# Issuing the value matmuls of a latent attention two key tiles at a time

## The chip, the cores and the metric

One Trainium2 chip, one of its cores. The metric is the device time of one execution in microseconds (us); the kernel before was run three times.

## The reference

Four pairs of an attention-like layer and a feed-forward-like layer on x of shape (2, 1024, 256) with a context of shape (2, 77, 256). The change touches only the first attention ("latent attention", stage A of the kernel), in which x supplies the queries and both the context and x itself supply keys and values:

```python
q = ln @ Wq                                   # ln: normed x, 1024 rows in each of 2 batches
kv = concatenate([xn, ln], axis=-2) @ Wkv     # xn: normed context, 77 rows; 1101 keys
k, v = split(kv, 2, axis=-1)                  # 16 heads of 64
logits = einsum('bhld,bhsd->bhls', q * scale, k * scale)
w = softmax(logits)
out = einsum('bhls,bhsd->bhld', w, v)
out = out.transpose(0, 2, 1, 3).reshape(B, L, INNER) @ Wo
```

## The kernel before, in words

Stage A takes some 1,130 us of the span; the stages behind it (three mixtures of experts, three other attentions, an alignment, soft slots) are untouched.

The stage runs 16 **units**, n = 0 to 15, one for each pair of heads (8) in each batch b (2). Each engine has its own queue, written out by hand, and they meet at semaphores. In a unit the 1101 keys are walked in KT = 9 **key tiles** kt (eight of 128, the last of 77). Scores are made with keys on the partitions and 1024 queries on the free axis, so that a key tile of two heads j makes four **halves** of 512 queries; a half is two matmuls (L395, L397) into one of three PSUM banks, and ScalarE takes it through Exp into `probs` (L483). `probs` is a ring of RING = 3 key tiles.

- **TensorE (PE)**, `body` (L368), in order: for each key tile the four halves, and behind them work for the same or other units. `values(n, b, kt)` (L337) waits until a key tile's four halves are through Exp and issues its four matmuls (L344: two blocks of 512 queries by two heads; each is a 64-column matmul in f32, in the trace two records and two weight loads, so 8 records for a key tile) into banks 4 and 5, where they accumulate over the nine key tiles. Before the change `values(kt - 1)` follows the halves of key tile kt, and `values(KT - 1)` closes the unit. `denominators` (L350, matmuls L356) then sums `key_sums` over partitions, again with 64 columns.
- Between the halves PE also does the work of the **next unit** m = n + 1: `project_q` at kt 0 (L270), `project_k` and `project_ctx` at (2, 0) (L270, L290, L293), `project_v` at kt 2, j = 1 (L302; it waits for `k_lo` from VectorE), and from kt 3 on two **maxima** pieces behind each half (`more`, L376; matmul L316): 48 pieces of 367 keys, whose largest score VectorE finds. They go through three banks, so a piece waits until the third one back is reduced. Behind the last piece `rows(m)` (L320) turns the maxima over. At kt 1 the output projection of the unit before, `leave` (L324, matmuls L333), has its two parts c = 0 and 1.
- **VectorE (DVE)**: the low parts of q (L512) and copies (L515), adding the output of the unit before to x (`add`, L543, which releases `x_added`), the low part of k (L521, releases `k_lo`), copies of k (L529, releases `k_second`), 48 reductions (L532), one over their results (L535), and the division by the denominator (`heads`, L555).
- **ScalarE (ACT)**: the exponentials, the high parts of q and k (L441, L446), copies of v (L456), the DMA that lays the maxima's rows out (L462), and Ln and Exp of the denominators (L498, L501) after `denominators`. `project_q` of the next unit waits for that Ln.
- **GpSimd (POOL)**: one addition for each head and key tile from kt 1 on into `key_sums` (L587), 16 in a unit. ScalarE may overwrite a place in the ring only when the values and the sum that read it are done (L478, L479).

`project_k` of unit m of 2 and more waits for `x_added` (L284), so for the second `add` of unit n - 1. Unit 0 has no `leave`; unit 15 has no next unit, so no projections and no maxima.

Of the kernel before, what the change touches and what calls it, by code (L numbers as in the profile page):

```python
# [171 lines left out]
def wait(engine, semaphore, value):  # L172

    if not isinstance(value, int) or value > 0:
        engine.wait_ge(semaphore, value)


def latent_attention(nc, consts, x, a, ctx_n, w_qkv, w_o, slots_zeroed):
# [14 lines left out]
    KT = S // P + 1  # L193
    QT = S // P
    UNITS = 2 * QT
    RING = 3
    assert PIECE * 3 == KEYS and PIECE % 2
    OWN = [slice(0, DH), slice(DH, P)]
    OTHER = [slice(DH, P), slice(0, DH)]
# [4 lines left out]
    with ExitStack() as stack:  # L204
# [7 lines left out]
        v_tok = sc.sb("v_tok", [P, 2, KT, P])  # L212
        probs = sc.sb("probs", [P, 2, RING, S])
        key_sums = sc.sb("key_sums", [P, 2, S])
# [51 lines left out]
        def _(pe):  # L266
# [7 lines left out]
            def project_q(m, b):  # L274
                if b == 0:
                    pe.wait_ge(s["in_loaded"], 8 * m + 16)
                wait(pe, s["logden_ready"], 2 * m - 2)
                project(0, b).then_inc(s["q_ps"], 1)

            def project_k(m, b):  # L280
                if isinstance(m, int) and m < 2:
                    pe.wait_ge(s["q_lo"], 2 * m + 2)
                else:
                    pe.wait_ge(s["x_added"], 2 * m - 2)  # L284
                project(1, b).then_inc(s["k_ps"], 1)

            def project_ctx(m, b):

                for c in range(C):
                    pe.matmul(ps[:, 3, 0:CTX], wqkv[:, 1, c, :], ctx_n[:, c, b * CTX:(b + 1) * CTX],  # L290
                              start=c == 0, stop=c == C - 1)
                for c in range(C):
                    mm = pe.matmul(ps[0:CTX, 3, P:2 * P], ctx_n[:, c, b * CTX:(b + 1) * CTX], wqkv[:, 2, c, :],  # L293
                                   start=c == 0, stop=c == C - 1)
                mm.then_inc(s["ctx_ps"], 1)

            def project_v(m, b):

                pe.wait_ge(s["k_lo"], 2 * m + 2)
                for kt in range(KT - 1):  # L300
                    for c in range(C):
                        mm = pe.matmul(bank_pair(6)[:, kt * P:(kt + 1) * P], a[:, c, b * S + kt * P:b * S + (kt + 1) * P],  # L302
                                       wqkv[:, 2, c, :], start=c == 0, stop=c == C - 1)
                mm.then_inc(s["v_ps"], 1)

            def maxima(m, b, first, count):

                for i in range(first, min(first + count, PIECES)):
                    j, qt = divmod(i // 3, QT)
                    if i == 0:  # L310
                        pe.wait_ge(s["k_second"], 2 * m + 2)
                    elif i < 3:
                        pe.wait_ge(s["v_ready"], m + 1)
                    else:
                        pe.wait_ge(s["piece_max"], PIECES * m + i - 2)
                    pe.matmul(ps[:, MAX_BANKS[i % 3], 0:PW], q_one[:, b, j, qt * P:(qt + 1) * P],  # L316
                              k_one[:, b, j, (i % 3) * PIECE:(i % 3) * PIECE + PW], start=True, stop=True)\
                      .then_inc(s["piece_ps"], 1)

            def rows(m):  # L320
                pe.wait_ge(s["nmax_ready"], m + 1)
                pe.transpose(ps[0:UNITS, 7, 0:P], nmax[:, :], consts["ident"][:, :]).then_inc(s["rows_ps"], 1)

            def leave(n, c, q_after=None):  # L324

                if c == 0:
                    pe.wait_ge(s["heads_ready"], n + 1)
                    if q_after is not None:
                        pe.wait_ge(s["q_lo"], 2 * q_after + 2)
                else:  # L330
                    pe.wait_ge(s["x_added"], 2 * n + 1)
                for blk in range(2):
                    mm = pe.matmul(ps[:, 6 + blk, :], wo[:, c * P:(c + 1) * P], heads[:, blk * BLK:(blk + 1) * BLK],  # L333
                                   start=True, stop=True)
                mm.then_inc(s["y_ps"], 1)

            def values(n, b, kt):  # L337

                pe.wait_ge(s["exp_ready"], 4 * KT * n + 4 * kt + 4)
                if kt == 0:  # L340
                    wait(pe, s["heads_ready"], n)
                for blk in range(2):
                    for j in range(2):
                        mm = pe.matmul(ps[DH * j:DH * j + DH, 4 + blk, :], v_tok[:, b, kt, DH * j:DH * j + DH],  # L344
                                       probs[:, j, kt % RING, blk * BLK:(blk + 1) * BLK],
                                       start=kt == 0, stop=kt == KT - 1)
                        if (blk, j) == (1, 1):
                            mm.then_inc(s["pv_ps"], 1)
# [19 lines left out]
            def body(n, b, first, last):  # L368
                m, mb = n + 1, 1 - b
                if b == 1:  # L370
                    pe.wait_ge(s["out_loaded"], 8 * n + 8)
                pe.wait_ge(s["row_ready"], 32 * n + 32)
                pe.wait_ge(s["k_second"], 2 * n + 2)
                done = 0

                def more():  # L376

                    nonlocal done
                    if not last and kt >= 3 and done < PIECES:
                        maxima(m, mb, done, 1)  # L380
                        done += 1
                        if done == PIECES:
                            rows(m)

                for kt in range(KT):
                    kw = P if kt < KT - 1 else CTX
                    for j in range(2):
                        for blk in range(2):
                            cols = slice(blk * BLK, (blk + 1) * BLK)
                            half = 4 * kt + 2 * j + blk  # L390
                            if half >= 3:
                                pe.wait_ge(s["exp_ready"], 4 * KT * n + half - 2)
                            else:
                                wait(pe, s["exp_ready"], 4 * KT * n)
                            pe.matmul(ps[0:kw, half % 3, :], k_one[:, b, j, kt * P:kt * P + kw], q_one[:, b, j, cols],  # L395
                                      start=True, stop=False)
                            pe.matmul(ps[0:kw, half % 3, :], k_two[:, b, j, kt * P:kt * P + kw], q_two[:, b, j, cols],  # L397
                                      start=False, stop=True).then_inc(s["score_ps"], 1)
                            more()
                            more()  # L400
                        if (kt, j) == (0, 0) and not last:
                            project_q(m, mb)
                        if kt == 1 and not first:
                            leave(n - 1, j, None if last else m)
                        if (kt, j) == (2, 0) and not last:
                            project_k(m, mb)
                            project_ctx(m, mb)
                        if j and kt:
                            values(n, b, kt - 1)
                        if (kt, j) == (2, 1) and not last:  # L410
                            project_v(m, mb)
                if not last:
                    kt = KT
                    while done < PIECES:
                        more()
                values(n, b, KT - 1)
                if last:
                    pe.wait_ge(s["x_added"], 2 * n)
                denominators(n)
                if last:  # L420
                    leave_last(n)
# [10 lines left out]

            pe.wait_ge(s["zeroed"], 7)
            units(pe, body, prologue)

        @block.scalar
        def _(act):
# [34 lines left out]
            def body(n, b, first, last):  # L472
                m, mb = n + 1, 1 - b
                for kt in range(KT):
                    kw = P if kt < KT - 1 else CTX
                    for j in range(2):
                        if kt >= RING:
                            act.wait_ge(s["pv_ps"], KT * n + kt - RING + 1)  # L478
                            act.wait_ge(s["summed"], 2 * (KT - 1) * n + 2 * max(kt - RING, 1))  # L479
                        for blk in range(2):  # L480
                            half = 4 * kt + 2 * j + blk
                            act.wait_ge(s["score_ps"], 4 * KT * n + half + 1)
                            act.activation(probs[0:kw, j, kt % RING, blk * BLK:(blk + 1) * BLK], ps[0:kw, half % 3, :],  # L483
                                           ACT.Exp, scale=1.0 / 8.0).then_inc(s["exp_ready"], 1)
# [2005 lines left out]
```

## Time and profile before

| | |
|---|---|
| median of 3 runs | 4280.51 us (4279.39 to 4281.56) |
| profiled execution, its own time | 4283.65 us |
| its span | 4281.7 us |
| PE busy | 3114.4 us (73%) |
| DVE busy | 2152.2 us (50%) |
| ACT busy | 1510.2 us (35%) |
| POOL busy | 1037.0 us (24%) |

The busy shares are means over all stages. What a change to stage A is worth has to be read inside one of its units, from the order of the timeline there and from which wait ends last. A record of a matmul shows a modelled end; starts, and the gap from one weight load to the next, are the better measure. "PE" rows are matmuls, "PEld" rows weight loads.

### The profile page before, as it was taken

The numbers are of one execution on the slowest core, as the hardware profiler recorded it, in microseconds if no ns is written. First come the engines' busy times: TensorE is split into PE (matmuls) and PEld (weight loads), VectorE is DVE, ScalarE is ACT, GpSimd is POOL, SyncE is SP. The second block draws the span as 40 slices with busy tenths as digits, with TensorE's granted clock in tenths as the row PEclk, the third lists the DMA queues.
The fourth block names the chain that finished last, engine by engine and source line by source line (L and its number), as shares of the span: only waits on it lengthen the run. The fifth ranks groups of instructions, "written<-read, shape, count | busy, mean of one in ns | idle before, by whom it ended". The sixth has DMA issues, their size and how long they took to land. (4 is left out here: it accounts for less than half of the span.)

```text
span 4281.7 us, 41469 instructions
## 1 busy us (share of the span) xinstructions
PE 3114.4 (73%) x14046; PEld 1867.5 (44%) x14046; DVE 2152.2 (50%) x3679; ACT 1510.2 (35%) x2290; POOL 1037.0 (24%) x625
## 2 busy tenths in 40 slices
PE   4899999999965576397585888988469530069769
PEld 1554545455434343397252444443259510034344
DVE  3655556555513262376364767765247543721270
ACT  2344444444433234264132344555236210022230
POOL 0355556455532120301131000000220312001110
PEclk7899999999977787698697899999679765579899
DMA  2000000000004200464100000000056324110260
GB/s 84 4 6 1 5 5 5 5 0 5 2 10 143 63 1 1 149 219 140 34 0 10 3 2 3 5 2 1 31 180 221 101 23 52 6 24 30 81 234 20
DMA packets 92601, 204.72 MB, mean 48 GB/s; under 512 B 31146, under 2 KB 65578, under 8 KB 83739
## 3 DMA queue, kind: packets, MB, share of 16 engines
q0 software_dynamic: 18512, 109.48, 7.5%
q1 hardware_dynamic: 69946, 86.94, 7.5%
q10 hardware_dynamic: 3984, 6.29, 0.4%
q8 instruction: 88, 1.44, 0.1%
q14 instruction: 71, 0.57, 0.0%
HBM read 154.41 MB, written 48.01 MB: 47 GB/s over the span
## 5 line engine op out<-in xcount | busy, mean ns | idle before, releaser
L587 POOL TENSOR_TENSOR A_key_sums<-A_key_sums,A_probs 128x1024 f32<-128x1024 f32 (+1 forms) x224 | 526.9, 2372 | 253.4 <-ACT A_probs L483 253.4
L483 ACT ACTIVATE A_probs<-A_banks 128x512 f32<-128x512 f32 (+1 forms) x576 | 329.4, 597 | 413.2 <-PE A_banks L397 411.0
L532 DVE TENSOR_REDUCE A_part_max<-A_banks 128x1 f32<-128x367 f32 x768 | 354.0, 531 | 156.8 <-PE A_banks L316 155.4
L1629 ACT ACTIVATE F_probs<-F_banks 128x512 f32<-128x512 f32 x512 | 272.1, 601 | 356.9 <-PE F_banks L1577 343.0
L1686 DVE TENSOR_REDUCE F_part_max<-F_banks 128x1 f32<-128x512 f32 x512 | 319.2, 684 | 47.3 <-PE F_banks L1533 46.5
L395 PE MATMUL A_banks<-A_q_one,A_k_one 128*128 128x512 f32 (+1 forms) x576 | 256.8, 446 | 26.7 <-ACT A_probs L483 23.3
L344 PE MATMUL A_banks<-A_probs,A_v_tok 128*64 128x512 f32 x1152 | 275.6, 604 | 0.0
L1533 PE MATMUL F_banks<-F_k_split,F_q_split 128*128 128x512 f32 x512 | 233.3, 480 | 35.6 <-DVE F_k_split L1678 34.1
L316 PE MATMUL A_banks<-A_k_one,A_q_one 128*128 128x368 f32 x768 | 230.0, 382 | 6.8 <-ACT A_v_tok L456 6.4
L1577 PE MATMUL F_banks<-F_q_split,F_k_split 128*128 128x512 f32 x512 | 211.2, 444 | 23.7 <-ACT F_probs L1629 19.4
L1996 PE MATMUL G_banks<-G_path,G_ctx_rows 77*128 77x512 f32 x16 | 14.0, 1071 | 294.2 <-DMA G_ctx_rows<-in_G_ctx_rows 294.2
L397 PE MATMUL A_banks<-A_q_two,A_k_two 128*128 128x512 f32 (+1 forms) x576 | 227.3, 395 | 0.0
L161 POOL TENSOR_SCALAR F_r<-F_r,F_ln_w 128x512 f32<-128x512 f32 x16 | 28.8, 1818 | 786.6 <-DVE F_r L126 786.6
L316 PEld LDWEIGHTS A_banks<-A_k_one,A_q_one 128*128 128x128 f32 x768 | 147.3, 192 | 94.6 <-DVE A_part_max L532 58.4
L1533 PEld LDWEIGHTS F_banks<-F_k_split,F_q_split 128*128 128x128 f32 x512 | 100.6, 201 | 181.0 <-DVE F_part_max L1686 112.6
L395 PEld LDWEIGHTS A_banks<-A_q_one,A_k_one 128*128 128x128 f32 (+1 forms) x576 | 106.5, 185 | 140.0 <-issue 96.0
L1546 PE MATMUL F_banks<-F_probs,F_v_tok 128*32 128x512 f32 x1024 | 149.4, 658 | 15.9 <-ACT F_probs L1629 15.9
L270 PE MATMUL A_banks<-g_y,A_wqkv 128*128 128x512 f32 x256 | 122.2, 622 | 30.7 <-DVE A_part_max L570 26.0
L587 POOL TENSOR_TENSOR A_key_sums<-A_probs 128x1024 f32<-128x1024 f32 x32 | 75.9, 2373 | 281.5 <-ACT A_probs L483 281.5
L834 PE MATMUL F_banks<-F_y_hi,F_w_split 128*128 128x256 f32 x736 | 130.1, 290 | 11.9 <-DVE F_w_split L993 11.9
L834 PE MATMUL D_banks<-D_y_hi,D_w_split 128*128 128x256 f32 x736 | 130.1, 290 | 11.9 <-DVE D_w_split L993 11.9
L1996 PEld LDWEIGHTS G_banks<-G_path,G_ctx_rows 77*128 77x128 f32 x16 | 5.2, 335 | 302.3 <-DMA G_ctx_rows<-in_G_ctx_rows 295.1
(532 smaller groups left out, 6432.0 us busy)
## 6 DMA issues: line engine op xcount, KB each, us to landing
H_w<-in_H_w SPq DMA_DIRECT2D x16, 1024.0 KB, 7.1
moe_in<-A_zeros ACTq DMA_DIRECT2D x1, 5888.0 KB, 17.4
D_tile_in<-moe_in SPq DMA_DIRECT2D x23, 256.0 KB, 5.4
moe_out<-D_z SPq DMA_DIRECT2D x23, 256.0 KB, 5.1
F_tile_in<-moe_in SPq DMA_DIRECT2D x23, 256.0 KB, 5.4
moe_out<-F_z SPq DMA_DIRECT2D x23, 256.0 KB, 5.0
slots<-H_staged SPq DMA_DIRECT2D x8, 512.0 KB, 4.1
made<-H_made POOLq DMA_DIRECT2D x16, 256.0 KB, 6.3
```

Of the source, the lines that this page charges most:

```text
L316: pe.matmul(ps[:, MAX_BANKS[i % 3], 0:PW], q_one[:, b, j, qt * P:(qt + 1) * P], k_one[:, b, j, (i % 3) * PIECE:(i % 3) * PIECE + PW], star ...
L344: mm = pe.matmul(ps[DH * j:DH * j + DH, 4 + blk, :], v_tok[:, b, kt, DH * j:DH * j + DH], probs[:, j, kt % RING, blk * BLK:(blk + 1) * BLK ...
L395: pe.matmul(ps[0:kw, half % 3, :], k_one[:, b, j, kt * P:kt * P + kw], q_one[:, b, j, cols], start=True, stop=False)
L397: pe.matmul(ps[0:kw, half % 3, :], k_two[:, b, j, kt * P:kt * P + kw], q_two[:, b, j, cols], start=False, stop=True).then_inc(s["score_ps" ...
L483: act.activation(probs[0:kw, j, kt % RING, blk * BLK:(blk + 1) * BLK], ps[0:kw, half % 3, :], ACT.Exp, scale=1.0 / 8.0).then_inc(s["exp_re ...
L532: dve.tensor_reduce(part_max[:, i // 3, i % 3:i % 3 + 1], ps[:, MAX_BANKS[i % 3], 0:PIECE], AX.X, ALU.max).then_inc(s["piece_max"], 1)
L587: pool.tensor_tensor(key_sums[0:kw, j, :], before, probs[0:kw, j, kt % RING, :], ALU.add).then_inc(s["summed"], 1)
L834: mm = pe.matmul(ps[:, 1 + pairs * (n % 2) + pair, at * SLOT:(at + 1) * SLOT], weight_in(i, w_part, pair, c, QM * q + at), part[:, i % 2, ...
L1533: mm = pe.matmul(bank, q_split[:, mb, hd // 2, qt * P:(qt + 1) * P], k_split[:, mb, hd, kb * BLK:(kb + 1) * BLK], start=True, stop=True)
L1577: pe.matmul(ps[:, k % 3, :], k_split[:, b, hd, kt * P:(kt + 1) * P], q_split[:, b, hd // 2, blk * BLK:(blk + 1) * BLK], start=True, stop=T ...
L1629: act.activation(probs[:, i % RING, hd, :], ps[:, k % 3, :], ACT.Exp, scale=DH ** -0.5).then_inc(s["exp_ready"], 1)
L1686: op = dve.tensor_reduce(part_max[:, i // QB, i % QB:i % QB + 1], bank, AX.X, ALU.max)
```

## The change

The value matmuls of two key tiles are issued together, behind the halves of key tiles 3, 5 and 7, and those of the last three key tiles at the end of the unit. Since a key tile's probabilities are then read up to three key tiles later, the ring holds six of them. No instruction is added or removed.

```diff
@@ -193,7 +193,9 @@
-    RING = 3
+    RING = 6
+    VALUES_BEHIND = {3: (0, 1), 5: (2, 3), 7: (4, 5)}
+    VALUES_LAST = (6, 7, 8)
@@ -405,15 +407,17 @@
                             project_k(m, mb)
                             project_ctx(m, mb)
-                        if j and kt:
-                            values(n, b, kt - 1)
+                        if j:
+                            for done_kt in VALUES_BEHIND.get(kt, ()):
+                                values(n, b, done_kt)
                         if (kt, j) == (2, 1) and not last:
                             project_v(m, mb)
                 if not last:
                     kt = KT
                     while done < PIECES:
                         more()
-                values(n, b, KT - 1)
+                for done_kt in VALUES_LAST:
+                    values(n, b, done_kt)
```

## Rows read from the trace of the kernel before

**Rows 1.** Windows: stage A; us, then busy (instructions) by engine, PE clock, DMA.

```profile
95.00:1210.00 1115.00, 1025.03 (x4225) 551.38 (x4225) 612.06 (x1005) 490.25 (x780) 602.79 (x256) 0.98 0.01 4
```

**Rows 2.** Groups by line, stage A: count, busy, mean ns, idle before and releaser.

```profile
L587 POOL TENSOR_TENSOR A_key_sums<-A_key_sums,A_probs 128x1024 f32<-128x1024 f32 (+1 forms) x224 | 526.9, 2372 | 253.4 <-ACT A_probs L483 253.4
L532 DVE TENSOR_REDUCE A_part_max<-A_banks 128x1 f32<-128x367 f32 x768 | 354.0, 531 | 156.8 <-PE A_banks L316 155.4
```

**Rows 3.** Timeline of VectorE, the heads multiplication that closes each unit: start, us.

```profile
482.88 1.22 DVE L555 TENSOR_TENSOR A_heads<-A_banks,A_rden 128x1024 f32<-128x1024 f32 x1 [8.55 <-ACT A_rden L501]
552.38 1.22 DVE L555 TENSOR_TENSOR A_heads<-A_banks,A_rden 128x1024 f32<-128x1024 f32 x1 [8.55 <-ACT A_rden L501]
620.18 1.23 DVE L555 TENSOR_TENSOR A_heads<-A_banks,A_rden 128x1024 f32<-128x1024 f32 x1 [8.55 <-ACT A_rden L501]
...
1165.79 1.23 DVE L555 TENSOR_TENSOR A_heads<-A_banks,A_rden 128x1024 f32<-128x1024 f32 x1 [8.45 <-ACT A_rden L501]
1216.59 1.23 DVE L555 TENSOR_TENSOR A_heads<-A_banks,A_rden 128x1024 f32<-128x1024 f32 x1 [42.32 <-ACT A_rden L501]
```

**Rows 4.** Timeline, one key tile in the stretch of the maxima, all engines.

```profile
521.67 0.19 PEld L395 LDWEIGHTS A_banks<-A_q_one,A_k_one 128*128 128x128 f32 x1 [0.81 <-issue]
...
522.61 3.66 DVE L532 TENSOR_REDUCE A_part_max<-A_banks 128x1 f32<-128x367 f32 x8 [1.88 <-PE A_banks L316]
...
524.00 4.72 POOL L587 TENSOR_TENSOR A_key_sums<-A_key_sums,A_probs 128x1024 f32<-128x1024 f32 x2 [0.83 <-ACT A_probs L483]
...
525.35 1.94 PE L344 MATMUL A_banks<-A_probs,A_v_tok 128*64 128x512 f32 x8
...
527.22 0.19 PEld L395 LDWEIGHTS A_banks<-A_q_one,A_k_one 128*128 128x128 f32 x1 [0.81 <-issue]
```

**Rows 5.** Timeline, the end of a unit and the next one's first score.

```profile
608.41 4.68 POOL L587 TENSOR_TENSOR A_key_sums<-A_key_sums,A_probs 77x1024 f32<-77x1024 f32 x2 [0.80 <-ACT A_probs L483]
...
611.18 3.65 PE L344 MATMUL A_banks<-A_probs,A_v_tok 128*64 128x512 f32 x16
...
614.67 1.89 PE L356 MATMUL A_banks<-A_key_sums,g_ones 128*64 128x512 f32 x8
...
616.48 0.19 PEld L395 LDWEIGHTS A_banks<-A_q_one,A_k_one 128*128 128x128 f32 x1 [0.81 <-issue]
```

**Rows 6.** Timeline, key tiles 1 and 2: from the output projection to `project_k`.

```profile
629.93 1.98 PE L333 MATMUL A_banks<-A_heads,A_wo 128*128 128x512 f32 x4 [1.96 <-DVE g_x L543]
...
631.85 1.94 PE L344 MATMUL A_banks<-A_probs,A_v_tok 128*64 128x512 f32 x8
631.96 1.22 DVE L543 TENSOR_TENSOR g_x<-g_x,A_banks 128x1024 f32<-128x1024 f32 x1 [2.08 <-PE A_banks L333]
...
633.71 0.19 PEld L395 LDWEIGHTS A_banks<-A_q_one,A_k_one 128*128 128x128 f32 x1 [0.81 <-issue]
...
634.75 3.60 PE L270 MATMUL A_banks<-g_y,A_wqkv 128*128 128x512 f32 x8
```

**Rows 7.** Timeline, key tile 2 to the first maxima piece.

```profile
639.43 2.48 DVE L521 TENSOR_TENSOR A_k_one<-A_banks,A_k_one 64x1024 fp32r<-64x1024 f32 x2 [6.25 <-ACT A_k_one L446]
...
639.73 0.39 PE L397 MATMUL A_banks<-A_q_two,A_k_two 128*128 128x512 f32 x1
...
641.96 3.65 PEld L302 LDWEIGHTS A_banks<-A_wqkv,g_y 128*128 128x128 f32 x32 [0.86 <-DVE A_k_one L521]
...
646.13 0.19 PEld L316 LDWEIGHTS A_banks<-A_k_one,A_q_one 128*128 128x128 f32 x1 [0.30 <-DVE A_k_two L529]
```

**Rows 8.** Windows of PE alone: us, busy (instructions), PE clock, DMA.

```profile
490.00:492.00 2.00, 0.68 (x3) 1.00 0.00 0
492.00:494.00 2.00, 1.37 (x2) 0.66 0.00 0
```

**Rows 9.** Timeline of the last unit: GpSimd's sums and the denominators.

```profile
1176.74 32.62 POOL L587 TENSOR_TENSOR A_key_sums<-A_key_sums,A_probs 128x1024 f32<-128x1024 f32 x14 [3.00 <-ACT A_probs L483]
...
1209.46 3.61 PE L356 MATMUL A_banks<-A_key_sums,g_ones 128*64 128x512 f32 x8 [4.86 <-issue]
```

## The prediction

> **What bounds the kernel now.** I began with the windows of stage A. PE is busy 1025 of 1115 us, against 612 for DVE, 603 for POOL and 490 for ACT [rows 1]. That invites the reading that PE sets the pace and that any drained or reordered matmul counts. But a matmul's busy time contains waits, so I went on to the groups by line: DVE's reductions are idle 155.4 us waiting for PE's maxima pieces, and POOL's sums 253.4 us for ACT's probabilities [rows 2]. So DVE and PE wait for each other, and only the order in one unit tells which wait counts where.
>
> The timeline of DVE gives the unit. The heads multiplications of units 4, 5 and 6 start at 482.88, 552.38 and 620.18: one unit of 69.50 us and one of 67.80 [rows 3]. Of the 14 distances between the heads of units 0 and 14, ten are of the short kind and four of the long. The last unit takes 50.80.
>
> Then I read one unit in four places.
>
> *The stretch of the maxima* (key tiles 3 to 8). A key tile takes 527.22 - 521.67 = 5.55 us. In it DVE does eight reductions without a gap, 3.66 us, and is idle 1.88 [rows 4]. PE's scores and pieces run from 521.67 to the values' start at 525.35, 3.68 us, which is just what DVE's reductions allow: PE is paced by DVE there, and DVE stands still only while the values pass. POOL works 4.72 of the 5.55 and is idle 0.83.
>
> *The end of the unit.* From the first values matmul at 611.18 to the next unit's first weight load at 616.48 PE has three tiles' worth of 64-column matmuls in a row: values of key tiles 7 and 8 and the denominators [rows 5]. 5.30 us for three, and 631.85 to 633.71, 1.86 us, for one that stands alone [rows 6]: so one tile streams in (5.30 - 1.86)/2 = 1.72 us and leaving the 64-column form costs 0.14. POOL's last sums end at 608.41 + 4.68 = 613.09, before the denominators start at 614.67. So nothing but the values stands ahead of the denominators, and everything of the next unit (Ln, `project_q`, scores) stands behind them.
>
> *Key tiles 1 and 2.* The second part of `leave` starts at 629.93; the add that follows runs 631.96 to 633.18, and `project_k` waits for it. It starts only at 634.75, because values(0) and two halves stand ahead of it [rows 6].
>
> *Before `project_v`.* The scores' last matmul starts at 639.73, then values(1) pass, and the weight load of `project_v` waits until 641.96 for DVE's low part of k, done at 639.43 + 2.48 = 641.91 [rows 7]. So values(1) lie wholly in a wait that ends later by itself. Before it was a free place.
>
> **The change, part by part**, for a middle unit (1 to 14).
>
> *values(0) leave key tile 1.* The next wait there is the add. PE needs 0.05 us to go on behind DVE (from 641.91 to 641.96 [rows 7]), so `project_k` can start at 633.23 in place of 634.75. The halves of key tile 2 take 634.75 - 633.71 = 1.04 and fit between the end of `leave` and then. Gain 1.5. Bounds: 0, if another wait takes its place, and 1.86, the whole tile.
>
> *values(1) leave key tile 2.* They were covered by the wait for `k_lo`. The wait stays, moved up by the 1.5 above, as ACT's and DVE's work on k hangs on `project_k` alone. Gain 0. PE now stands idle from about the end of the scores (some 0.2 us behind 639.73, moved up) to `project_v`: about 1.95 us.
>
> *The stretch of the maxima.* Five separate value tiles (2 to 6, behind key tiles 3 to 7) become three groups of two (0 to 5). DVE's idle time was 5 x 1.88 = 9.40. A group of two stands 1.72 longer: 3 x (1.88 + 1.72) = 10.80. Cost 1.40. Between key tiles 4 and 5, and 6 and 7, nothing interrupts the reductions: 16 in a row at 3.66 per eight. So the time that merging saves is the 0.16 by which 1.88 exceeds a tile's stream, twice, while a sixth tile comes in for 1.72. Bounds for a group: 3.44 (two streams and nothing else) and 3.76 (twice 1.88), so a cost of 0.92 to 1.88.
>
> *The end of the unit* has three value tiles where it had two: 1.72. This is on the path by rows 5. Its lower bound is 0, were something else to end there last, but POOL has 1.58 us in hand and more afterwards: in a pair of key tiles without a gap POOL falls 2 x (4.72 - 3.66) behind, about 2.1 us, and the group of two that follows gives 3.6 back, so it enters key tile 8 without a backlog.
>
> *The ring of six.* It removes ACT's wait for values(kt - 3) and POOL's sum. ACT is busy 490 of 1115 us [rows 1] and in the stretches that I read it is PE's scores that it waits for, so alone the ring gives nothing; without it the later values would stall ACT. Cost 0. No DMA is moved; ACT's row DMA and the reload of weights keep their places, since v and q projections stay where they were.
>
> Sum of a middle unit: -1.5 + 0 + 1.40 + 1.72 = +1.62. Fourteen of them: +22.7.
>
> *Unit 0* has no add to wait for; all of values(0) goes, with its switch: -1.9 + 1.40 + 1.72 = +1.2.
>
> *Unit 15* has no maxima. POOL is its bound: 14 sums in a row for 32.62 us, from 1176.74 to 1209.36, then the denominators at 1209.46, for which PE had waited 4.86 [rows 9]. The scores of key tile 2 come earlier by values(0), and with them POOL's row of sums: -1.9. One more value tile at its end fits into those 4.86 us.
>
> *The clock.* The unit of 69.50 us holds a second part of `leave` that was slow: the granted clock is 1.00 in 490 to 492, where PE is busy 0.68 of 2 us, and 0.66 over 492 to 494, so it fell from 2.4 to 1.2 GHz behind that wait of 1.96 us [rows 8]. It costs 69.50 - 67.80 = 1.70. Four of the 14 units show it. The change makes a second idle place of the same length before `project_v`, which is on the path of the first maxima piece (the piece waits 0.30 for L529 only [rows 7]). I take it to be hit as often as the first: 4 x 1.70 = 6.8. Bounds: 0, and all 15, 25.5.
>
> Sum: 22.7 + 1.2 - 1.9 + 6.8 = +28.8. The profiled execution took 4283.65 for a span of 4281.7, and lies 3.1 over the median; on its own scale the forecast is 4312.5, on that of the median 4280.5 + 28.8 = **4309 us**, 0.67% slower.
>
> **The rivals.** *A: it does what the order suggests, fewer changes between full-width and 64-column matmuls.* A middle unit enters the 64-column form eight times before, and four after. If PE set the pace everywhere and no tile lay in a free place, the tiles would cost the same as before and 4 x 0.16 x 16 = 10 us would go: 4270. For it speaks PE's busy share; against it, DVE's idle time exactly at the values and PE's idle time before `project_v`. It decides if a group of two idles DVE less than (9.40 + 1.5 - 1.72)/3 = 3.06 us, and two tiles stream for 3.44. The Trainium skill, "TensorEngine Tiling (Array Packing)", Tiling Modes, has the rule that changing the tiling mode drains TensorE, which speaks for A; it gives no price, and the trace shows the drain as small (0.14 and 0.16).
>
> *B: the end of the unit hides the added tile,* because the layout of the maxima rows by DMA or POOL's late sums come to end last there. Then a middle unit is -1.5 + 1.40, nothing, and the whole -3 to +4, with the clock's 6.8 or without: about 4281. POOL's end at 613.09 speaks against it.
>
> *C: the clock falls in nearly every unit* before `project_v`, and at `leave` more often. 22.0 + 25.5 = +47.5: 4328. For it: PE is then idle some 1.95 and 1.96 us within some eleven; against: ten of 14 units pass a wait of 1.96 at full clock.
>
> **How the numbers follow.** Forecast 0.80, A 0.09, B 0.07, C 0.04. The lowest of the forecast is a middle unit of -1.86 + 0.92 + 1.72 = +0.8, without the clock's term: some +10, 4290. The highest is +1.88 for the groups, a head gain of only about 1, the clock's +6.8 and a few more falls: +45, 4326. That is the range. A change of under 0.2% (8.6 us) is not told from none. Slower 0.84 (forecast and C), same 0.07 (B), faster 0.09 (A).
>
> **What the profile after would show.** In a middle unit: `project_k` 0.05 behind the add's end; the load of `project_v` with a wait of 2 us or more for L521; 16 reductions of L532 in a row, idle 3.6 before them; 32 records of L344 and L356 from the last maxima to the next unit's scores, 7.0 us in place of 5.3; heads 69.4 us apart, and 71.1 where the clock fell. In the last unit POOL's row of sums 1.9 earlier. The forecast is wrong if groups of two idle DVE about 3.0 us, if the denominators wait for L587 in middle units, or if heads are under 68 apart.

## The result and the profile after

| | before | after |
|---|---|---|
| median | 4280.51 us | 4300.89 us (4300.11 to 4303.98) |
| profiled execution, its span | 4281.7 us | 4298.3 us |
| stage A, first score of unit 0 to heads of unit 15 | 1074.7 us | 1096.8 us |
| middle units (14), the short kind | 67.8 us, ten | 69.3 us, seven |
| middle units, the long kind | 69.4 to 69.6 us, four | 70.2 to 70.95 us, seven |
| last unit | 50.80 us | 48.82 us |

The changed kernel is slower by a ratio of 1.0051 (95% interval 1.0036 to 1.0065): 20 us, where 29 were forecast. In the lines of the profile after, L346 is the values, L335 `leave`, L536 the reductions, L559 the heads, L591 POOL's sums, L397 and L399 the scores.

The units, by DVE's heads multiplication (timeline of the kernel after; rows 3 are those of before):

```profile
558.28 1.23 DVE L559 TENSOR_TENSOR A_heads<-A_banks,A_rden 128x1024 f32<-128x1024 f32 x1 [10.27 <-ACT A_rden L505]
629.21 1.23 DVE L559 TENSOR_TENSOR A_heads<-A_banks,A_rden 128x1024 f32<-128x1024 f32 x1 [10.26 <-ACT A_rden L505]
698.52 1.23 DVE L559 TENSOR_TENSOR A_heads<-A_banks,A_rden 128x1024 f32<-128x1024 f32 x1 [10.27 <-ACT A_rden L505]
...
1188.72 1.23 DVE L559 TENSOR_TENSOR A_heads<-A_banks,A_rden 128x1024 f32<-128x1024 f32 x1 [10.17 <-ACT A_rden L505]
1237.54 1.23 DVE L559 TENSOR_TENSOR A_heads<-A_banks,A_rden 128x1024 f32<-128x1024 f32 x1 [40.35 <-ACT A_rden L505]
```

A long unit (70.93), a short one (69.31) and the last (48.82). Now the short one, from 629.21, place by place. First the start of `project_k` (L272) behind the add and of `project_v` (L304) behind the low part of k, then the first maxima piece (L318), in PE's weight loads:

```profile
642.26 0.30 PEld L272 LDWEIGHTS A_banks<-g_y,A_wqkv 128*128 128x128 f32 x2 [0.82 <-DVE g_x L547]
...
649.58 3.65 PEld L304 LDWEIGHTS A_banks<-A_wqkv,g_y 128*128 128x128 f32 x32 [2.29 <-DVE A_k_one L525]
653.74 0.19 PEld L318 LDWEIGHTS A_banks<-A_k_one,A_q_one 128*128 128x128 f32 x1 [0.29 <-DVE A_k_two L533]
```

`project_k` comes 642.26 - 629.21 = 13.05 behind the heads, in place of 634.75 - 620.18 = 14.57 [rows 3, 6]. It now waits for the add (done at 642.21, 0.05 earlier, as forecast), which was not what held it before. `project_v` comes 20.37 behind them for 21.78, and its load waits 2.29 us for L525 where it had waited 0.86 [rows 7]: that is the free place, now empty. The first piece is 24.53 behind the heads, for 25.95: 1.42 gained.

The stretch of the maxima on VectorE (timeline after; rows 4 for one key tile of before):

```profile
654.21 0.54 DVE L536 TENSOR_REDUCE A_part_max<-A_banks 128x1 f32<-128x367 f32 x1 [0.53 <-PE A_banks L318]
655.01 3.41 DVE L536 TENSOR_REDUCE A_part_max<-A_banks 128x1 f32<-128x367 f32 x7 [0.25 <-PE A_banks L318]
662.02 7.23 DVE L536 TENSOR_REDUCE A_part_max<-A_banks 128x1 f32<-128x367 f32 x16 [3.61 <-PE A_banks L318]
672.85 7.23 DVE L536 TENSOR_REDUCE A_part_max<-A_banks 128x1 f32<-128x367 f32 x16 [3.60 <-PE A_banks L318]
683.63 3.66 DVE L536 TENSOR_REDUCE A_part_max<-A_banks 128x1 f32<-128x367 f32 x8 [3.55 <-PE A_banks L318]
```

Three idle times of 3.61, 3.60 and 3.55 stand where five of 1.88 were, and between them 16 reductions run without a gap. Sixteen take 7.23, not 2 x 3.66: a joined run saves 0.09. So the stretch costs 10.76 - 9.40 - 2 x 0.09 = 1.18 more.

The end of the unit (timeline after, PE; rows 5 for before):

```profile
687.59 0.28 PE L324 MATMUL A_banks<-g_ident,A_nmax 128*16 128x128 f32 x1 [1.15 <-DVE A_nmax L539]
687.80 5.37 PE L346 MATMUL A_banks<-A_probs,A_v_tok 128*64 128x512 f32 x24
...
693.00 1.89 PE L358 MATMUL A_banks<-A_key_sums,g_ones 128*64 128x512 f32 x8
...
694.81 0.19 PEld L397 LDWEIGHTS A_banks<-A_q_one,A_k_one 128*128 128x128 f32 x1 [0.81 <-issue]
```

From the first value matmul to the next unit's first score 7.01 us, for 5.30: 1.71 more. POOL's last sums of this unit run from 685.02 to 689.71, well ahead of the denominators at 693.00. -1.42 + 1.18 + 1.71 = 1.47, and the short units differ by 1.5.

The long unit that began at 698.52 has its fall of the clock in `project_v`, behind the wait of 1.85 us ahead of it (PE alone, windows of the kernel after, and the matmuls of `project_v` there):

```profile
716.00:718.00 2.00, 1.03 (x5) 1.00 0.00 0
718.00:720.00 2.00, 1.13 (x10) 1.00 0.00 0
720.00:722.00 2.00, 2.00 (x12) 0.50 0.00 0
722.00:724.00 2.00, 2.00 (x14) 0.64 0.00 0
```
```profile
718.87 5.46 PE L304 MATMUL A_banks<-A_wqkv,g_y 128*128 128x128 f32 x32 [1.85 <-DVE A_k_one L525]
```

`project_v` takes 5.46 us for the 3.84 that it takes elsewhere in this trace. Three of the seven long units have their fall there, at a price of 1.6. The other four have it in the second part of `leave`, at 0.9 to 1.1. It comes late in that part there and goes on over the scores, as in the long unit of 70.40 us that holds these two rows (timeline; at full clock the first takes 1.98 and the second 0.79):

```profile
288.89 2.78 PE L335 MATMUL A_banks<-A_heads,A_wo 128*128 128x512 f32 x4 [1.96 <-DVE g_x L547]
290.69 1.41 PE L397 MATMUL A_banks<-A_q_one,A_k_one 128*128 128x512 f32 x1
```

A short unit waits 0.39 us for the add behind those scores, and in a long one that wait is used up. I read this as a part of why the price is lower; no run tests it.

Last, POOL in the last unit (rows 9 for before):

```profile
1197.61 32.63 POOL L591 TENSOR_TENSOR A_key_sums<-A_key_sums,A_probs 128x1024 f32<-128x1024 f32 x14 [0.93 <-ACT A_probs L487]
```

The same row of 14 sums, beginning 8.89 behind the heads of unit 14 where it had begun 10.95 behind: the unit is 2.0 shorter.

### The profile page after: what moved, and what is told of

Same layout as the page of the kernel before. It is cut to its first block and busy times, and to the rows that moved or that the text cites. A ratio compares the mean times of both kernels' runs of the same rounds, so it can differ in the third digit from the quotient of the medians.

```text
span 4298.3 us, 41337 instructions
## 1 busy us (share of the span) xinstructions
PE 3098.8 (72%) x14046; PEld 1876.8 (44%) x14046; DVE 2148.8 (50%) x3679; ACT 1508.7 (35%) x2290; POOL 1035.1 (24%) x625
## 5 line engine op out<-in xcount | busy, mean ns | idle before, releaser
L591 POOL TENSOR_TENSOR A_key_sums<-A_key_sums,A_probs 128x1024 f32<-128x1024 f32 (+1 forms) x224 | 525.2, 2371 | 253.0 <-ACT A_probs L487 253.0
L536 DVE TENSOR_REDUCE A_part_max<-A_banks 128x1 f32<-128x367 f32 x768 | 351.2, 531 | 182.6 <-PE A_banks L318 181.2
L397 PE MATMUL A_banks<-A_q_one,A_k_one 128*128 128x512 f32 (+1 forms) x576 | 260.6, 452 | 26.6 <-ACT A_probs L487 23.2
L346 PE MATMUL A_banks<-A_probs,A_v_tok 128*64 128x512 f32 x1152 | 261.3, 598 | 0.0
L318 PE MATMUL A_banks<-A_k_one,A_q_one 128*128 128x368 f32 x768 | 232.0, 385 | 7.2 <-ACT A_v_tok L460 6.9
L399 PE MATMUL A_banks<-A_q_two,A_k_two 128*128 128x512 f32 (+1 forms) x576 | 229.0, 398 | 0.0
L161 POOL TENSOR_SCALAR F_r<-F_r,F_ln_w 128x512 f32<-128x512 f32 x16 | 28.8, 1813 | 784.4 <-DVE F_r L126 784.4
L318 PEld LDWEIGHTS A_banks<-A_k_one,A_q_one 128*128 128x128 f32 x768 | 147.4, 192 | 98.8 <-DVE A_part_max L536 63.8
L397 PEld LDWEIGHTS A_banks<-A_q_one,A_k_one 128*128 128x128 f32 (+1 forms) x576 | 107.5, 187 | 105.6 <-issue 60.9
L591 POOL TENSOR_TENSOR A_key_sums<-A_probs 128x1024 f32<-128x1024 f32 x32 | 75.8, 2372 | 305.5 <-ACT A_probs L487 305.5
L272 PE MATMUL A_banks<-g_y,A_wqkv 128*128 128x512 f32 x256 | 124.2, 630 | 34.6 <-DVE A_part_max L574 26.0
L346 PEld LDWEIGHTS A_banks<-A_probs,A_v_tok 128*64 128x64 f32 x1152 | 77.0, 136 | 139.3 <-issue 136.0
```

The lines of the kernel that those rows point to most:

```text
L536: dve.tensor_reduce(part_max[:, i // 3, i % 3:i % 3 + 1], ps[:, MAX_BANKS[i % 3], 0:PIECE], AX.X, ALU.max).then_inc(s["piece_max"], 1)
L591: pool.tensor_tensor(key_sums[0:kw, j, :], before, probs[0:kw, j, kt % RING, :], ALU.add).then_inc(s["summed"], 1)
```

## The experiments

The account above is a sum of places: a value tile costs 1.72 us where nothing else is waited for, nothing in a wait that ends later anyway, and grouping saves a quarter of a microsecond for each group less. The runs below move one tile or one group at a time. All but the two with fillers do the whole computation and nothing else; "before" in a ratio is the kernel before, run on the same chip beside them. The experiments ran on three chips. So where two of them are compared, I also give stage A of their profiled executions, measured as in the table above: 1074.7 us before and 1096.8 after. From the heads of unit 15 to the end the instructions are the same in all eleven kernels, and yet that part took anything from 3056.5 to 3069.0 us, so some us of any difference between medians can come from there.

**The ring alone.** `RING = 6`, every tile where it was.

> The ring of six alone, every value tile at its old place. Theory of places (a value tile costs 1.72 us wherever nothing else is waited for, and nothing where a wait covers it; merging saves only the small exit and entry of the 64-column form): no change from before, 4280 +- 3. Rival R, the larger ring itself costs (other addresses, probabilities read later): a good part of the 20 us that the change cost, 4290 or more.

4281.65 us, ratio 1.0002 (0.9993 to 1.0011). The ring costs nothing; its short units are 67.8 us and it has four long ones.

**Tile 6 from the end of the unit into the group before it.**

```diff
-    VALUES_BEHIND = {3: (0, 1), 5: (2, 3), 7: (4, 5)}
-    VALUES_LAST = (6, 7, 8)
+    VALUES_BEHIND = {3: (0, 1), 5: (2, 3), 7: (4, 5, 6)}
+    VALUES_LAST = (7, 8)
```

> The changed kernel with tile 6 moved from the end of the unit into the group behind key tile 7, so that the end has two tiles as before. Theory of places: both places are on the path, the end loses 1.72 and the stretch of the maxima gains 1.72, 4301 +- 4; in the last unit nothing. Rival B, the end of the unit has cover of its own: then taking a tile from it gives nothing and the stretch pays 1.72, 4301 + 26 = 4327. If the stretch had cover instead: 4275.

4301.62 us, ratio 1.0049 (1.0036 to 1.0063), the changed kernel's. DVE's idle time ahead of its last eight reductions (timeline):

```profile
684.45 3.66 DVE L536 TENSOR_REDUCE A_part_max<-A_banks 128x1 f32<-128x367 f32 x8 [5.28 <-PE A_banks L318]
```

5.28 for 3.55, 1.73 more, and the short units are 69.3 us and stage A 1096.7, as before the move. The two places cost the same and neither hides anything: rival B of the prediction is out.

**One tile back into the free place before `project_v`.**

```diff
-    VALUES_BEHIND = {3: (0, 1), 5: (2, 3), 7: (4, 5)}
+    VALUES_BEHIND = {2: (0,), 3: (1,), 5: (2, 3), 7: (4, 5)}
```

> The changed kernel with one tile put back into the free place: tile 0 behind key tile 2, ahead of the wait for the low part of k; tile 1 alone behind key tile 3; the rest as changed. Theory of places: 1.7 us less in the stretch of the maxima of each of 15 units, and the idle time before project_v is filled, so no clock falls there: 4301 - 26 - 3 = 4272 (4267 to 4279). Rival M or R: it has more groups than the changed kernel (five for four) and the same ring, so it stays at 4300 or above.

4275.99 us, ratio 0.9988 (0.9979 to 0.9997). This kernel has one group more in a unit than the changed one and the same ring, and is 25 us faster (stage A 1072.9, 23.9 less). Its short units are 67.6 us: 69.3 - 1.7. So the place, not the number of groups, decides. The clock did less well than expected: seven units are long (69.0 to 69.2), though now no fall is at `project_v`; all seven are at `leave`.

**Grouping without moving tiles 0 and 1.**

```diff
-    VALUES_BEHIND = {3: (0, 1), 5: (2, 3), 7: (4, 5)}
-    VALUES_LAST = (6, 7, 8)
+    VALUES_BEHIND = {1: (0,), 2: (1,), 5: (2, 3, 4), 7: (5, 6)}
+    VALUES_LAST = (7, 8)
```

> Values of key tiles 0 and 1 stay at their old places, 2 to 4 are issued together behind key tile 5, 5 and 6 together behind 7, 7 and 8 at the end as before. Five groups in a unit where before has eight. Theory of places: DVE's five idle times of 1.88 become 1.88 + 2 x 1.72 and 1.88 + 1.72, 8.92 for 9.40, and each run of reductions that is joined saves another 0.09: 0.75 us in each of 15 units, 4269 (4264 to 4274). Rival M, issuing in groups is itself what costs (DVE, POOL or ACT starved while a group passes): slower than before, by the 1.2 us of a unit that the stretch of the maxima gained, some 4295.

4280.93 us, ratio 1.0000 (0.9991 to 1.0009), stage A 1074.5: neither the 4269 nor the 4295 of the expectation. Its short units are 67.02 us, the 0.75 less that the places give, but there are only three of them. The other eleven are 68.6 to 68.8. Here is one of each, by the heads (timeline):

```profile
549.74 1.22 DVE L559 TENSOR_TENSOR A_heads<-A_banks,A_rden 128x1024 f32<-128x1024 f32 x1 [8.55 <-ACT A_rden L505]
618.45 1.22 DVE L559 TENSOR_TENSOR A_heads<-A_banks,A_rden 128x1024 f32<-128x1024 f32 x1 [8.55 <-ACT A_rden L505]
685.47 1.23 DVE L559 TENSOR_TENSOR A_heads<-A_banks,A_rden 128x1024 f32<-128x1024 f32 x1 [8.55 <-ACT A_rden L505]
```

And the place where the time goes (PE, the second part of `leave` in a long unit, and the windows around it):

```profile
490.83 3.32 PE L335 MATMUL A_banks<-A_heads,A_wo 128*128 128x512 f32 x4 [1.96 <-DVE g_x L547]
```
```profile
488.00:490.00 2.00, 0.87 (x4) 1.00 0.00 0
490.00:492.00 2.00, 1.17 (x2) 0.83 0.00 0
492.00:494.00 2.00, 2.00 (x3) 0.50 0.00 0
```

The same fall behind the same wait of 1.96 us as in rows 8, in eleven units rather than four. The falls are not scattered. In the 14 middle units the second part of `leave` takes 3.3, 3.7, 2.0 and 2.9 us, and then the same four again and again (2.0 is full clock). This was a reading of the trace; the next run tests whether the wait brings the falls.

**The same kernel with that wait filled.** The four value matmuls of tile 0 are issued once more ahead of the second part of `leave` (in `scrap`, with `start=True, stop=True`), and their results are overwritten.

```diff
+                        if (kt, j) == (1, 1) and not first:
+                            scrap(n, b)
                         if kt == 1 and not first:
                             leave(n - 1, j, None if last else m)
```

> The kernel with tiles 0 and 1 at their old places and 2 to 6 in two groups, and with the four value matmuls of tile 0 issued once more, ahead of the second part of leave; their result is overwritten by the real ones, so this is work for nothing put into PE's wait of 1.96 us. Theory of the clock (the time that grouping saves is eaten because PE's clock falls at that wait in 11 of 14 units rather than in 4): no fall is left, every middle unit 67.0 us, 4281 - 11 x 1.66 = 4263 (4259 to 4268). Rival, the long units come from something else, such as the order: 4281, or some us more for the added work.

4259.43 us, ratio 0.9937 (0.9923 to 0.9951). Thirteen of 14 middle units are 67.0 to 67.1 us, as expected. Adding work that nobody needs took 15.4 us off stage A (1074.5 to 1059.1): 16.8 in the middle units, less 1.5 that the last unit is longer (52.27 for 50.80). The medians differ by 21 and the ratio gives 27; what goes beyond stage A lies where the instructions are the same and is not the filler's. The granted clock over 220 to 1100 us is 1.00, where it was 0.98 without the filler. So the wait itself was harmless, the clock behind it was not. PE's `leave` matmuls over 220 to 1100 us, without the filler and with it (groups by line, one kernel each):

```profile
L335 PE MATMUL A_banks<-A_heads,A_wo 128*128 128x512 f32 x98 | 61.4, 759 | 24.9 <-DVE g_x L547 23.6
```
```profile
L335 PE MATMUL A_banks<-A_heads,A_wo 128*128 128x512 f32 x104 | 52.4, 626 | 2.7 <-DVE A_q_two L527 0.2
```

**The changed kernel with both waits filled** (the line above, and another `scrap` at (2, 1) ahead of `project_v`).

> The changed kernel with four value matmuls for nothing (tile 0, overwritten later) ahead of the second part of leave and again ahead of project_v, so that both of PE's waits of about 1.95 us are filled with work that takes 1.86. Theory of the clock: the seven long units of the changed kernel (70.2 to 70.9 us for 69.3) become short, 4301 - 9 = 4292 (4288 to 4297), and 12 us are left over the kernel before, 21 us of longer units less that kernel's own four falls. Rival, the long units have another cause, or the fillers stick out of the waits: 4301 or more.

4297.91 us, ratio 1.0031 (1.0021 to 1.0042). The median is outside what was expected by 1 us, but the kernel before ran 2 us higher beside it (4282.46), and by the ratio the kernel is 13 us slower than before, where 12 were expected. Stage A is 1090.8 us, 6.0 less than in the changed kernel. Thirteen of the 14 middle units are 69.2 to 69.4 us, the other is 70.96. So the changed kernel's long units come from the clock too. The 13 us are not the price of the order alone: they are its 21 us (14 units of 69.3 for 67.8) less the 6.7 us of four falls that only the kernel before still has. Of the change's 20 us the order accounts for nearly all and the clock for the small rest, since before and after both pay for falls.

**A useful tile in the wait.** The kernel before (ring of six), with values(0) ahead of the second part of `leave` and no longer behind key tile 1:

```diff
+                        if (kt, j) == (1, 1):
+                            values(n, b, 0)
                         if kt == 1 and not first:
                             leave(n - 1, j, None if last else m)
```

> The kernel before (ring of six, one tile behind each key tile) with values(0) issued ahead of the second part of leave, into PE's wait of 1.96 us for the add, rather than behind it. Theory of places: project_k starts 1.5 us earlier behind its add, no tile becomes dearer, and the wait at which the clock fell is gone: 14 x 1.5 + 6.8 = 28 us less, 4253 (4249 to 4260). Rival A, only the number of changes of form counts (it stays at eight in a unit): no change, 4281.

4252.94 us, ratio 0.9929 (0.9916 to 0.9942). Thirteen middle units of 66.3 to 66.5 us, one of 67.92. Stage A is 1050.4 us, 24.3 less than before; the places and the clock had given 28. Eight groups in a unit, as before; only the place of one changed.

**Tile 7 into the wait for the last reductions.** The kernel before (ring of six); in the last unit, which has no maxima, the tile stays behind the halves.

```diff
                         if done == PIECES:
+                            values(n, b, 7)
                             rows(m)
```

> The kernel before (ring of six) with values(7) issued ahead of the transpose of the maxima rather than behind it, into PE's wait of 1.4 us for VectorE's last reductions. Theory of places: 1.1 us less in each of 15 units (1.4 less one more change of form), 4264 (4260 to 4272). Rival: the rows of the maxima are laid out 0.5 us later, and if that DMA or POOL's last sums then end last, the gain is halved or less: 4272 to 4280. Rival A: one more change of form, 4283.

4279.26 us, ratio 0.9991 (0.9983 to 1.0000), 15 us above the expectation; stage A is 1074.8. The denominators start at 613.32, 0.51 behind POOL's last sum, and the next scores are not late. What failed is the clock again: the one short middle unit is 66.75, 1.05 less than before as expected, and thirteen are 68.3 to 68.5. Here too there is a rhythm: over the first six middle units the second part of `leave` grows from 3.02 to 3.66 us, by 0.12 to 0.14 a unit. The `leave` matmuls show it (groups by line, 220 to 1100 us):

```profile
L335 PE MATMUL A_banks<-A_heads,A_wo 128*128 128x512 f32 x98 | 61.6, 760 | 24.8 <-DVE g_x L550 23.5
```

**All of it**: values(0) ahead of the second part of `leave`, 1 in the free place, 2 to 6 in one group behind key tile 7, 7 ahead of `rows`, 8 at the end.

> Both placements together, and values 2 to 6 in one group behind key tile 7. Theory of places: 1.5 + 1.1 + 1.0 (one idle time of DVE of 1.88 + 4 x 1.72 = 8.76 for five of 9.40, four joins of 0.09) = 3.6 us less in 14 units and 2.1 in unit 0, and the fall of the clock at leave gone, 4281 - 52 - 7 = 4222 (4215 to 4235). Rival: POOL, 5.3 us behind after five key tiles without a gap, delays the denominators: 4240 or more.

4223.06 us, ratio 0.9863 (0.9849 to 0.9877): it beats both kernels, and the forecast of 4222 holds to 1 us. Stage A is 1018.9 us, 55.8 less than before, where 59 were forecast. VectorE and POOL in a unit (timelines):

```profile
423.65 17.67 DVE L541 TENSOR_REDUCE A_part_max<-A_banks 128x1 f32<-128x367 f32 x39 [0.25 <-PE A_banks L318]
450.02 3.66 DVE L541 TENSOR_REDUCE A_part_max<-A_banks 128x1 f32<-128x367 f32 x8 [8.70 <-PE A_banks L318]
```
```profile
424.86 23.43 POOL L596 TENSOR_TENSOR A_key_sums<-A_key_sums,A_probs 128x1024 f32<-128x1024 f32 x10 [3.87 <-ACT A_probs L492]
451.41 4.69 POOL L596 TENSOR_TENSOR A_key_sums<-A_key_sums,A_probs 77x1024 f32<-77x1024 f32 x2 [3.12 <-ACT A_probs L492]
```

40 reductions in a row, one idle time of 8.70, and POOL, which falls behind over five key tiles, has caught up 3.12 us before the last one. Thirteen middle units are 64.25 to 64.4 us, the fourteenth is 65.74.

## Why the prediction was right, and where its size was off

| term | forecast | measured |
|---|---|---|
| values(0) leave key tile 1 | -1.5 | -1.42 to the first piece |
| values(1) leave the free place | 0 | 0, `project_v` still released by L525 |
| stretch of the maxima | +1.40 | +1.18 |
| a third tile at the end | +1.72 | +1.71 |
| middle unit, short kind | +1.62, of 14: 22.7 | +1.50, of 14: 21.0 |
| unit 0 | +1.2 | +0.8 |
| last unit | -1.9 | -2.0 |
| clock | +6.8 | +2.3 |
| sum in stage A | +28.8 | +22.1 |

*The reading that DVE and PE wait for each other, with PE paced in the stretch of the maxima,* held. A group of two idles DVE 3.59 on average, where rival A needed less than 3.06. The small miss in this term is the 0.09 of a joined run of reductions, which rows of eight could not show. As to A, grouping does save something: from eight groups to five takes 0.75 us off a short unit (67.02). Three joined runs of reductions are 0.27 of that, so TensorE's own part is some 0.16 a group, the prediction's figure. The Trainium skill, "TensorEngine Tiling (Array Packing)", Tiling Modes, has changes of tiling mode drain TensorE; by that rule the saving has the right sign. Whether it is that drain, no run shows. The 0.16 us a group stand against 1.72 for a tile in the wrong place.

*That values(1) had been free, and values(0) worth less than their length,* held, and is the cause of the loss: one tile moved into the free place, and 25 us go. *That the end of the unit has no cover* held (the run with tile 6 moved).

*The clock's term* was mis-sized, and is 4.5 of the 6.7 us by which the sum is too high. It took the rate of falls at the one wait, four in 14 units, for the rate at the second, and left the first alone: eight falls at 1.70, against four before. Measured are seven long units: four falls at `leave`, at 0.9 to 1.1 only, and three at `project_v` at 1.6. The three cost 4.9 us where 6.8 were forecast, and the four cost 4.1 where before they cost 6.7, which the forecast had left unchanged. By the distances of the heads, long over short is 979.2 - 14 x 69.30 = 9.0 us after and 955.9 - 14 x 67.80 = 6.7 before, so +2.3. That the count at the second wait, three of 14, came out near the forecast four was luck, as the rate can't be carried from one order to another: at the same wait of 1.96 us it is 4 of 14 units before and 7, 11 and 13 in three of the experiments (one tile back, grouping without tiles 0 and 1, tile 7). Within each kernel the falls keep a rhythm, every second unit in the changed one, three of every four in the grouped one; what sets it was not tested beyond filling the wait.

The stages behind A are the same instructions; the medians differ by 20.4 and stage A by 22.1, within the spread of those stages.

## What to carry to other kernels

Price a moved instruction by the place that it leaves and the place that it enters: in a wait that ends later by itself it is free, elsewhere it costs its whole length, and that outweighed by far what grouping saves. Look for the waits of the busiest engine first and put work that is ready there; the version that fills them and then groups the rest takes 1.4% off. And where TensorE waits for some 2 us in every round, as in this kernel, look for clock falls behind the wait, and fill it before anything else is tuned.

## What the runs showed of the hardware that was not expected

- Four matmuls for nothing in every unit made stage A 15.4 us shorter (1074.5 to 1059.1): in place of a wait of 1.96 us they kept TensorE at 2.4 GHz (granted clock 1.00 over 220 to 1100 us, 0.98 without them).
- With that wait open, the share of units with a fall went from 4 of 14 to 11 and 13 of 14 when a unit became 0.75 or 1.05 us shorter in another place, and took back the whole gain. The falls recur in a rhythm and not at random. In this kernel, orders that differ by under 2 us in a unit can't be compared without counting the falls.
- Sixteen reductions in a row take 7.23 us and eight take 3.66, so each break in a row costs VectorE 0.09 us besides the idle time.
